# A graph network on one core: first-transition products taken source by source, and the adjacency build run as two streams

## The reference

```python
agg = jax.ops.segment_sum(x[src], dst, num_segments=N_NODES)
agg = agg / jnp.maximum(cnt, 1.0)[:, None]
out = agg @ Wl.T + bl + x @ Wr.T
```

## Time and profile before

| | |
|---|---|
| median of three | 2687.6 us |
| profiled execution, its own time | 2701.79 us |
| its span | 2699.3 us |
| build loop | 43.72 to 449.43 us of the span |
| passes 0 to 6 | about 450 to 1300 us |
| attention | the rest |

### The profile page before, as it was taken

How to read it: one execution, slowest core, us unless ns; L and a number is a source line. 1 busy time by engine, 2 the same in 40 slices (tenths; PEclk the granted TensorE clock), 3 DMA queues, 4 the chain that set the end, 5 groups by cost and what they waited for, 6 DMA issues and landing times.

```text
span 2699.3 us, 48165 instructions
## 1 busy us (share of the span) xinstructions
PE 1760.8 (65%) x10229; PEld 1109.4 (41%) x10229; DVE 1418.9 (53%) x4461; ACT 1042.0 (39%) x3014; POOL 1025.5 (38%) x1355
## 2 busy tenths in 40 slices
PE   2666665699899999989355555645554555555554
PEld 0111111355555565656244444534344444444443
DVE  8888887433656533346244444534344444444444
ACT  3888886432554322212123223323223222233233
POOL 2000001322544310111455555565555655655552
PEclk9999999999999999999566666666666666666766
DMA  1000000100111101013433333333333333333331
GB/s 65 0 0 0 0 0 20 43 26 29 50 51 53 50 27 32 29 60 102 141 96 109 110 96 107 110 104 106 95 103 112 109 94 102 107 100 108 109 94 45
DMA packets 148866, 188.65 MB, mean 70 GB/s; under 512 B 25795, under 2 KB 117316, under 8 KB 148804
## 3 DMA queue, kind: packets, MB, share of 16 engines
q0 software_dynamic: 38784, 105.96, 13.5%
q1 hardware_dynamic: 110020, 82.00, 9.5%
HBM read 162.82 MB, written 25.04 MB: 70 GB/s over the span
## 4 chain that ended last, share of the span: by engine, by line
another core or an unknown queue 20%; DVE 13%; issue 10%; PE 7%; ACT 1%; DVEq 0%; DMA 0%; ACTq 0%
DVE counts L1460 4%; DVE a_score L1463 3%; PE aq_bank L1335 3%; PE acc_bank L1354 3%; DVE counts L1468 1%; DVE a_clipped L1473 1%; DVE counts L1392 1%; PE ap_bank L1341 0%; PE ac_bank L1370 0%; PE ac_bank L1371 0%; DVE counts L1416 0%; DVE a_stat L1424 0%; ACT counts L1300 0%; DVE a_stat L1423 0%
## 5 line engine op out<-in xcount | busy, mean ns | idle before, releaser
L1265 POOL DMA_INDIRECT counts<-keys_values,a_index x808 | 783.3, 969 | 576.9 <-ACT a_index L1280 340.6
L776 PE MATMUL z_bank<-y_parts,counts 128*128 128x384 bf16 (+1 forms) x3750 | 665.7, 329 | 4.1 <-DMA y_parts<-in_L_gnn_bq 4.1
L1335 PE MATMUL aq_bank<-counts 128*128 128x128 bf16 x2424 | 291.9, 263 | 356.6 <-issue 340.5
L1460 DVE TENSOR_TENSOR counts<-aq_bank,counts 128x512 f32<-128x512 f32 x202 | 139.3, 690 | 720.8 <-remote 602.5
L1354 PE MATMUL acc_bank<-counts 128*128 128x136 f32 x1616 | 338.9, 366 | 215.7 <-DVE counts L1468 107.9
L776 PEld LDWEIGHTS z_bank<-y_parts,counts 128*128 (+1 forms) x3750 | 370.0, 99 | 238.6 <-issue 14.1
L1296 ACT ACTIVATE counts<-a_clipped 128x32 f32<-128x32 f32 x202 | 46.1, 228 | 919.2 <-DVE a_clipped L1473 774.8
L1354 PEld LDWEIGHTS acc_bank<-counts 128*128 128x128 f32 x1616 | 288.5, 257 | 255.6 <-DVE counts L1468 129.6
L1335 PEld LDWEIGHTS aq_bank<-counts 128*128 128x128 bf16 x2424 | 211.6, 119 | 416.6 <-issue 406.3
L496 PE MATMUL share_build<-right_build,left_build 128*128 128x300 bf16 x816 | 276.9, 443 | 128.5 <-DVE right_build L434 98.0
L462 ACT ACTIVATE square_build<-iota_b_build,low_build 128x128 bf16<-128x128 bf16 x682 | 237.9, 387 | 2.2
(11 more groups left out here) (153 smaller groups left out, 1871.1 us busy)
## 6 DMA issues: line engine op xcount, KB each, us to landing
counts<-group_rel_rows SPq DMA_DIRECT2D x34, 768.0 KB
counts<-keys_values,a_index POOLq DMA_INDIRECT x808
self_term<-s_out SPq DMA_DIRECT2D x150, 64.0 KB, 1.6
s_in<-self_term SPq DMA_DIRECT2D x150, 64.0 KB, 1.8
residual<-x_in SPq DMA_DIRECT2D x75, 64.0 KB, 1.6
counts<-query_parts SPq DMA_DIRECT2D x34, 96.0 KB
x_in<-in_x SPq DMA_DIRECT2D x50, 64.0 KB, 1.8
x_in<-residual SPq DMA_DIRECT2D x50, 64.0 KB, 1.8
```

What stands on the lines that cost most here:

```text
L776: yield s, nc.tensor.matmul(bank(p, dt)[:, 0:width], counts[:, bass.ds(dt.value(P) + s * NA, P)], y3[(p - 1) % 2][:, s, 0:width], start=s ...
L1265: nc.gpsimd.indirect_dma_start(rows_kv[:, j, c, :], None, v.kv, bass.IndirectOffsetOnAxis(index[:, j, c:c + 1], 0)).then_inc(gathered[j], 16)
L1335: ins = nc.tensor.matmul(q_bank[s.slot()][:, c * P:c * P + P], spread[:, g.slot(), (j * GC + c) * P:(j * GC + c) * P + P], queries[:, g.sl ...
L1460: nc.vector.tensor_tensor(prod[:, :].rearrange("p (c d) -> p c d", c=GC), q_bank[s.slot()][:, :].rearrange("p (c d) -> p c d", c=GC), rows ...
```

## The change

It has two parts. **Build:** the pairs go in groups of `GB` = 4, two pairs from the first half of the chunks and two from the second half, in turn (two streams), a turn of the loop holds two groups, and there are 102 groups. One VectorE instruction compares for eight chunks at once (2400 elements, bf16 keys, the chunk as innermost dimension of four). GpSimd computes `place - low` for six of the eight chunks in one instruction (768 elements, bf16); ScalarE squares those in one instruction in place, makes the squares of the other two as before, and applies one relu to all eight (1024 elements). The subtraction of a group waits until the comparison of the group before it has ended (`right_ready`) and until the relu two groups back has ended (`left_ready`). Squares, left and right sides are rings of two groups, `share` of eight banks. An add waits for the add before the last one only. Eight window starts are loaded a turn, behind the comparison. **Dense passes:** in pass 0 each step ends with four products, of the source tile four steps back into the banks of tiles 0 to 3 of pass 1; of every later transition the last five sources of the first four tiles are issued source by source (`finish_begun`), with the transposes behind them. Pass 2's `TURNED` is 4 and its `TURN_AT` (2, 8); a logarithm on ScalarE stands ahead of pass 0.

```diff
-UB = 12
+UB = 8
+GB = 4
-FILL = {0: (4, 3, 6), 1: (20, 4, 8), 2: (16, 4, 14), 3: (12, 4, 16), 4: (10, 4, 8), 5: (10, 4, 8)}
-TURNED = {0: 2, 1: 1, 2: 3, 3: 2, 4: 1, 5: 1, 6: 2}
-TURN_AT = {1: (17, 24), 2: (20, 24), 3: (17, 24), 4: (17, 24), 5: (17, 24), 6: (6, 13)}
+FILL = {1: (20, 4, 8), 2: (10, 4, 10), 3: (12, 4, 16), 4: (10, 4, 8), 5: (10, 4, 8)}
+TURNED = {0: 2, 1: 1, 2: 4, 3: 2, 4: 1, 5: 1, 6: 2}
+TURN_AT = {1: (17, 24), 2: (2, 8), 3: (17, 24), 4: (17, 24), 5: (17, 24), 6: (6, 13)}
...
+            def differences(g):
+                g.count(pool, right_ready)
+                (g - 1).count(pool, left_ready)
+                lows = low_b[:, 0:2 * STREAM].rearrange("p (h m) -> p h m", h=2)[:, :, bass.ds(g.value(GB), BY_POOL)]
+                nc.gpsimd.tensor_tensor(square[:, g.slot(), :, :].rearrange("p (h c) n -> p h c n", h=2)[:, :, 0:BY_POOL, :],
+                                        place.unsqueeze(1).unsqueeze(1).to_broadcast([P, 2, BY_POOL, P]),
+                                        lows.unsqueeze(3).to_broadcast([P, 2, BY_POOL, P]), ALU.subtract).then_inc(diff_ready, 1)
...
-            nc.vector.tensor_scalar(key[:, :], key[:, :], float(-MID), None, ALU.add).then_inc(keys_ready, 1)
+            chain.step(nc.vector.tensor_copy(low_b, low[:, :]))
+            nc.vector.tensor_scalar(key_b, key[:, :], float(-MID), None, ALU.add).then_inc(keys_ready, 1)
...
+            def sides(g):
+                keys = key_b[:, 0:2 * STREAM].rearrange("p (h m) -> p h m", h=2)[:, :, bass.ds(g.value(GB), GB)]
+                nc.vector.tensor_tensor(right[:, g.slot(), :, :, :], iota_wide[:, :, :].unsqueeze(1).to_broadcast([P, 2, KW, 4]),
+                                        keys.unsqueeze(2).to_broadcast([P, 2, KW, 4]), ALU.is_equal).then_inc(right_ready, 1)
+
+            def turn(k, last=False):
+                for j in range(UB // GB):
+                    if not (last and j == UB // GB - 1):
+                        sides(Num(j + 1, k, UB // GB))
...
+                    for i in range(GB):
+                        q = Num(GB * j + i, k, UB)
+                        (q + 1).count(dve, mm_done)
+                        (q + 1).count(dve, column_sums)
...
+            def squares(g):
+                (g - 1).count(act, left_ready)
+                both = square[:, g.slot(), :, :].rearrange("p (h c) n -> p h (c n)", h=2)
+                for h in range(2):
+                    chunk = bass.ds(g.value(GB) + h * STREAM + BY_POOL, 1)
+                    nc.scalar.activation(both[:, h, BY_POOL * P:GB * P], place, ACT.Square, bias=low[:, chunk],
+                                         scale=-1.0).then_inc(squares_ready, 1)
+                (g + 1).count(act, diff_ready)
+                nc.scalar.activation(both[:, :, 0:BY_POOL * P], both[:, :, 0:BY_POOL * P], ACT.Square).then_inc(squares_ready, 1)
+
+            def one_hot(g):
+                act.wait_ge(squares_ready, g.value(3) + 3)
+                if g.c > 1:
+                    act.wait_ge(mm_done, (g - 1).value(GB))
+                nc.scalar.activation(left[g.slot()][:, :, :], square[:, g.slot(), :, :], ACT.Relu, bias=one[:, :],
                                      scale=-1.0).then_inc(left_ready, 1)
 
+            def step(g):
+                squares(g + 1)
+                one_hot(g)
...
+            def source_for_first_tiles(d):
+                (d + 1).count(pe, y_ready)
+                for n in range(AHEAD):
+                    nc.tensor.matmul(z_bank[n][:, 0:YW + 1], counts[:, bass.ds(d.value(NA) + n * P, P)],
...
+            def finish_begun(p, first):
+                for source in range(first, NT):
+                    pe.wait_ge(y_ready, NT * (p - 1) + source + 1)
+                    for n in range(AHEAD):
+                        ins = product(p, Num(n), source)
+                        if source == NT - 1:
+                            ins.then_inc(z_ready, 1)
...
+                if begun:
+                    stage(lambda d: transpose(p, d), dt, TURNED[p])
+                    stage(lambda d: products(p, d), dt, TURNED[p])
+                    return
...
+                    if p == 0 and not by_edge:
+                        stage(source_for_first_tiles, dt, PEELED - 1)
...
+            if 0 in passes and not by_edge:
+                chain.step(nc.scalar.activation(stat[:, 0, LOG1:LOG1 + 1], one[:, :], ACT.Ln))
```

More of the change, by code:

```diff
@@ L452, in _ @@
+            sides(Num(0))
+            with dve.Fori(0, TB - 1) as k:
+                turn(k)
+            turn(TB - 1, True)
         @block.scalar
@@ L826, in step @@
                         return
-                    filling = dt.k is None and NT <= dt.c and p < 6 and not by_edge
+                    filling = dt.k is None and NT <= dt.c and 0 < p < 6 and not by_edge
                     if filling and dt.c == NT:
@@ L941, in step @@
                         stage(lambda d: turned(p, d), dt, TURNED[p])
-                    stage(lambda d: second(p, d), dt, last)
+                    stage(lambda d: second(p, d), dt, max(last, TURNED[p]) if p < 6 else last)
                     stage(lambda d: sum_squares(p, d), dt, 0)
```

143 lines of the change are left out of this document (66 added, 77 removed).

## The result

The changed kernel takes 2810.7 us (median of 4 runs, 2798.95 to 2817.25) against 2690.5 us of the kernel before on the same chip: ratio 1.0431, 95% interval 1.0396 to 1.0465. It is some 120 us slower, where 15 us less was forecast and the range ended at 2700. Its profiled span is 2812.3 us, 113.0 more than before's.

The account below looks back on a forecast made before the run. VectorE was taken to set the build's pace, at 3.98 us per four pairs. Build +1, first transition -14 and later transitions -2 made -15, so 2672.6 us against the median; forecast's own range 2655 to 2690, 8-in-10 range 2605 to 2700.

Parts of the forecast that it names:

- The dense passes: Pass 0 and the transitions: a list of what is taken away and added, giving -14 us and, for later transitions, -2.
- the six cases: Whole kernel: forecast 0.38, GpSimd faster 0.32, no difference 0.12, slower by subtraction 0.08, by comparison 0.05, by port 0.05.
- Later transitions, -2: Transitions after the first: order even but for 0.7 us gained, table load -1.3, together -2 (-5 to +3).
- First transition, -14: Pass 0 to pass 1: tile 4's products begin at 531.9 against 545.9, -14 us (-20 to -2).
- Pass 0 was put at 2.5 us a tile: Pass 0 with four added products: 3.1 us a tile at 1.2 GHz, about 2.2 at 2.4 GHz, 2.5 taken.
- Tiles 1 and 2 I put 2.0 behind each other: Start of pass 1: transposes 2.0 us apart as all sums are there, tile 4's products 8.5 behind.
- Build, +1: The build: 3.97 us a group, ending at 450.4 against 449.4, +1 us (-40 to +100).
- the ring: Build, two groups long: relu, products, adds, comparison, subtraction, square, relu; 7.93 us, or 3.97 a group.
- The rival GpSimd at twice the rate: Build: GpSimd subtracts at the one-input rate as bf16 moves half the bytes; -40 - 14, about 2634 us; chance 0.32.
- The estimate of 1.8 us from the Trainium skill: Build: GpSimd's subtraction of 768 elements, estimated from 4497 ns for an add of 2048 f32.
- The table load, -1.3: Pass 2: the 1.28 us load before its first transpose moves to where ScalarE has nothing, -1.3 us.

Follow-up runs that it names:

- p2_as_before: The changed kernel with all of pass 2's numbers put back (turned 3 behind, after sources 20 and 24): 2706.1 us, 1.0052 of the kernel before.
- later_as_before: p2_as_before with the transitions to passes 2 to 6 tile by tile as in the kernel before: 2382.7 us, 0.9988 of the kernel before.
- sub_at_once: later_as_before without GpSimd's wait for the comparison in the build: 2646.9 us, 0.9801 of the kernel before.
- first_transition_only: later_as_before with the build of the kernel before: 2371.7 us, 0.9946 of the kernel before.

## Why the prediction was wrong

- **The step that failed: the list of "The dense passes".** It prices what is taken from and added to pass 0 and the transitions, and gives the later ones -2. The diff's third table, pass 2's `TURN_AT` (20, 24) to (2, 8) with `TURNED` 4 and the move of y on ScalarE, has no term at all. It costs some 98 us (pass 2 and the end of it, against p2_as_before), most of the 120. Without it the kernel is still 13 us slower than before (1.0052) and not 15 faster; that rest is the build and the later transitions, below. None of the six cases has it either. The row that would have shown it was there: in the kernel before, [0.17 <-ACT hT] with the sources up to 24, about 4 us, of cover. Moving the products to source 8 takes 16 sources (2.7 us at 0.167) of that cover away in each of 25 tiles; the wait became 3.19 us.
- **Later transitions, -2** (-0.7 for their order, -1.3 for the table load). The order costs about +15. The step "tile 0's sum is 12 products later, tiles 1 to 3's no longer wait for transposes" counted when sums come and not what TensorE does behind them. Its 2.0 us for tile 0 is right; the gain set against it is not there, as the transposes come 2.4 to 2.5 us apart in either order, and TensorE is at its slower level behind them.
- **First transition, -14.** It is -18.3 in the changed kernel and -15.2 with before's build, near the forecast by luck: two of its sizes were off in opposite directions. Pass 0 was put at 2.5 us a tile; it takes 3.1 at TensorE's lower level, as worked out, but only for the first tiles, and 1.9 at the faster one, where 2.2 was worked out. "Tiles 1 and 2 I put 2.0 behind each other": they come 4.8 apart (4.9 and 5.3 in before's trace, at 533.08, 537.99 and 543.30, where TensorE waited 2.37 us for `h` each time), so tile 4's products begin 15.2 us behind the last sources, not 8.5:

```profile
524.33 0.83 PE L806 MATMUL z_bank<-y_parts,counts 128*128 128x385 bf16 x4 [0.78 <-DVE y_parts L1099]
...
528.11 0.47 PE L783 MATMUL t_bank<-ident,h 128*128 128x128 f32 x1 [2.95 <-ACT h L953]
...
532.89 0.47 PE L783 MATMUL t_bank<-ident,h 128*128 128x128 f32 x1 [2.73 <-ACT h L953]
...
539.54 5.07 PE L806 MATMUL z_bank<-y_parts,counts 128*128 128x385 bf16 x18
```

- **Build, +1.** It is +12.7, with the ring right and its joints too short. Comparison 1.40 us (1.41 predicted), relu 1.13 (1.14), square 0.84 (0.92), subtraction 1.47 (1.6). The largest miss is from the products' start to the next comparison's: 2.92 us (299.04 to 301.96) for the 2.62 of the sum. The subtraction starts 0.26 behind the comparison's end (0.15 in the sum). 4.06 us a group in place of 3.97 is 9 of the 12 us, the later start of the first comparison (45.52, not 44.4) and the meeting at its start (last section) most of the rest. The register loads at a turn do delay the first add (1.47 us behind the products' start against 0.82), but the four adds then follow in 1.64 us instead of 2.07: 0.1 us a turn.
- **The rival GpSimd at twice the rate (0.32)** is wrong: 256, 512 and 768 bf16 elements take 0.61, 1.04 and 1.47 us, a line of 0.18 us and 1.68 ns an element, close to the 1.75 worked out from f32 rows. Half the bytes gave no double rate. The estimate of 1.8 us from the Trainium skill (GPSIMD Engine Reference, § 3.1) was 0.3 too long (plain proportion makes 1.7 of its 4497 ns): it amounts to 2.2 ns for an f32 element against 1.68 for a bf16 one here, and no run here shows whether the type makes that difference.
- **The table load, -1.3,** is gone from pass 2 as said (it stands at 463.55); pass 2's stretch in later_as_before is 1.4 us shorter than before's (130.89 against 132.25).

## What to carry to other kernels

Give each changed number of a schedule table a term of its own in the sum, and where it moves an instruction toward the front of a block, subtract the work that lay ahead of it from the wait it had: an instruction with 0.17 us of wait and 4 us of cover has no cover to give away. A greater distance between producer and consumer helps only when every in-order queue on the way (here ScalarE's copy, GpSimd's self term) and every buffer (the two slots of `h`) moves with it, and these limits hide behind each other, so that putting one right may show nothing. To bring the starts of four results together also brings their follow-up work together, where nothing is left to lie beside it.

## What the runs showed of the hardware

**GpSimd and VectorE shut each other out for whole instructions.** At the start of the changed kernel's build a subtraction starts inside a comparison and ends 1.32 us behind its end, nearly its own length:

```profile
45.52 2.73 DVE L452 TENSOR_TENSOR flat_build<-iota_wide_build,src_cols_build 128x2400 bf16<-128x2400 bf16 x2
...
47.00 2.57 POOL L381 TENSOR_TENSOR key_low_build<-iota_b_build,src_cols_build 128x768 bf16<-128x768 bf16 x1 [12.19 <-DVE flat_build L452]
```

In sub_at_once it is the comparison that comes second and grows from 1402 to 1979 ns. The adds, whose one input is in PSUM, ran beside a subtraction at their usual 0.47 us. The Trainium skill (SBUF — State Buffer, "Who interferes with whom") says just this of VectorE instructions with two SBUF inputs, and that the order of issue decides who waits; the runs agree in both directions. The changed kernel's wait for the comparison keeps the two apart in the loop, but it lies on the critical ring: without it the build was 52 us shorter (410.4 against 462.2).

**TensorE's level in pass 0.** The pair of weight products takes 1.22 us in before's pass 0 (the clock column shows 1.00 there all the same) and 0.70 us in the changed kernel from 483 us on, after the four products a tile had begun at 478 (granted clock 0.58 from 462 to 480, 0.65 to 483, 1.00 behind). In first_transition_only, whose build is before's, the faster level comes too, but two to three tiles later; there lie the 3 us between its 15.2 and the changed kernel's 18.3. In pass 2 the reverse: behind the 3.2 us wait the clock is 0.50 for 2.6 us and nine of the sources come 0.32 us apart instead of 0.17. So about 1.4 us of each long step is TensorE's slower level and not the wait itself.

The clock column alone doesn't tell the level. Between 100 and 380 us it reads 1.00 in the changed kernel's build and 0.50 in that of sub_at_once, which also lowers the mean clock of the whole run:

```profile
100.00:380.00 280.00, 157.62 (x552) 60.47 (x550) 215.88 (x346) 177.27 (x276) 101.41 (x69) 1.00 0.00 0
100.00:380.00 280.00, 178.70 (x625) 69.39 (x626) 273.50 (x394) 202.35 (x315) 114.84 (x79) 0.50 0.00 0
```

But eight products of 300 columns take 2.29 us in both. The spacing of known products is the better witness.

**The attention, which no kernel here changes, took two lengths.** From the last sum of pass 6 to the end it is 1411 us in before's trace and 1096 in that of later_as_before, with TensorE's granted clock at 0.66 and 0.76 and DMA at 105 and 136 GB/s between 1310 and 2280 us; build and passes agree in the two sessions within 0.1 us a step. Both lengths were met on the same chip. Which of the two numbers is cause, if either is, was not tried.
